# First feed-forward in plain float32: single products in place of high and low parts, and a fixed buffer for the routed up weights

## The chip, the cores and the metric

The kernel runs on one core of a Trainium2 chip. The metric is device time in microseconds (us); the time of a kernel is the median of its runs, and here there were three of the kernel before. The profile is one more execution, recorded by the hardware profiler.

## What is computed

Two transformer layers over 32 batches of 128 tokens with 128 features: cross-attention, then a feed-forward, twice. The change touches only the first feed-forward: a shared expert for every token, and eight routed experts of which each token uses the two with the highest scores.

```python
def _L0_ffn_ref(hidden_states, norm_weight, router_w, sw1, sb1, sw2, sb2, ew1, eb1, ew2, eb2):
    D, H, O, E, TOPK = (128, 512, 128, 8, 2)
    ...
    normed = hidden_states * jax.lax.rsqrt(var + 1e-08) * norm_weight
    shared = jnp.maximum(normed @ sw1 + sb1, 0.0) @ sw2 + sb2
    ...
    probs = jax.nn.sigmoid(flat @ router_w.T)
    scores, idx = jax.lax.top_k(probs, TOPK)
    w = scores / (jnp.sum(scores, axis=-1, keepdims=True) + 1e-06)
    ...
    h = jnp.maximum(jnp.einsum('td,edh->teh', flat, ew1) + eb1[None, :, :], 0.0)
    eo = jnp.einsum('teh,eho->teo', h, ew2) + eb2[None, :, :]
    routed = jnp.einsum('teo,te->to', eo, comb)
    return shared + routed.reshape(b, s, -1)
```

## The kernel before, in words

The program runs attention, the first feed-forward (`ffn0`, from L807), and then second attention and second feed-forward together. `P` is 128. The 32 batches form eight groups of four (512 tokens) and two halves of 16 batches. Each engine has its own block of code in `ffn0`, and semaphores order the engines; nothing reorders the instructions, so the order of an engine's work is the order of its code.

**Precision.** Each product of the feed-forward is three products of type float32r: `exact` (L1371) multiplies the high part of the weights by the high part of the data, low by high, and high by low. So each operand has to be split. ScalarE writes the high part (L1038 for weights, L1034 and L1096 for data, L1044 and L1111 for the hidden layer), and VectorE or GpSimd subtracts it from the whole for the low part (VectorE L1136 weights, L1259 and L1336 hidden layer, L1329 data of a block; GpSimd L967 data of a group). The weights come one expert after another through `w_in`, a buffer for two experts, so that SyncE's loads (L914) wait for VectorE's splits.

**Shared stage.** TensorE transposes a group (`transposes`, L1350), multiplies it by the shared up weights (`up`, L1381: a bias product and three of 512 columns for each of four slices of the hidden layer) and by the down weights (`down`, L1392: three of 512 columns each), then transposes the result back (`transpose_out`, L1404); VectorE adds it to `x` (`accumulate`, L1264). In the same stage the logits (L1367), the probabilities (ScalarE, L1060), the choice of two experts (VectorE `route`, L1159 to L1182), the place of each token in its expert's list (`prefix` on TensorE, `places` on VectorE, ending with the cast of `slots`, L1244) are made, once for each half. GpSimd makes the `scales` of a group (L959, L962) and scatters the normed rows into `xs` in DRAM, two indirect transfers a batch (L974); in its queue a group's scales stand behind three batches of scatters.

**Block stage.** 39 blocks of 128 rows for each half, 78 in all, each with one expert, whose number TensorE loads from `block_of` (L1478) to address the weights. SyncE loads blocks from `xs` in chunks of four. The loop of TensorE is four deep: transpose of block k (L1471), up of k-1 (bias L1481, three 512-column products L1483 to L1486), transposes of the hidden layer of k-2 (L1493), down of k-3 (four 256-column products L1504, a bias L1506, four 128-column products L1510). VectorE sums the two halves of the down product into `y_out` (L1343), and signals `by`. GpSimd scatters the second half while blocks of the first half run, each batch after a wait for `by` (L1011), and gathers the first half's results while blocks of the second half run, again each after a wait for `by` (L1018); VectorE adds them to `x` (L1311, L1316) at blocks that the list `ADD_AT` gives.

Of the kernel before, what the change touches and what calls it, by code (L numbers as in the profile page):

```python
# [89 lines left out]
class Kernel:  # L90
# [716 lines left out]
    def ffn0(self):  # L807
        nc, ps = self.nc, self.psum
        s = self.sems("f0", """small_in b2_rows sel tri iota b1_tr b2_tr b1_out b2_out b_hi b_rest b_mid b_low rows_zero
            rows_in w_hi w_lo stats mv veps scale xn xn_tr xT x_hi x_lo logit_mm prob  # L810
            top eq rank best m0 left m1 mask total rtot prefix scan small pos slot block_of
            s_rows up h_hi h_lo down out_copy out_tr acc
            bx_tr bx_hi bx_lo bup brelu bh_tr bh_hi bh_lo bdown by add0 add1""")
# [3 lines left out]
        experts_in = [self.sem(f"f0_experts_in{r}") for r in range(2)]  # L817
        UP_BANK, OUT_BANK, T_BANK, XT_BANK, PFX_BANK = 0, 4, 5, 6, 7
        U_BANKS, H_BANKS, X_BANKS, A_BANKS = (0, 1), (2, 3), (5, 6), (4, 7)
        XT_BANKS = (5, 4, 5, 4) + (XT_BANK,) * (G // 2)  # L820
        LOGIT_COL = 2 * E0 * HALF
        SH = E0
        W1_HI, W1_LO, W2 = 0, HID, 2 * HID
        xn = self.x_norm
        xT, outT = self.temp[:, 0:2], self.temp[:, 2]

        with ExitStack() as local:
# [4 lines left out]
            b2 = sb("b2", [NE, P])  # L832
            rw = sb("rw", [P, E0])
            nw = sb("nw", [P, 1])
            b2s = sb("b2s", [P, 1])
# [3 lines left out]
            b1_rows = sb("b1_rows", [P, E0, HID], BF16)  # L839
            b2_rows = sb("b2_rows", [P, E0, P], BF16)  # L840
            s_rows = sb("s_rows", [3, HID], BF16)
            sel3 = sb("sel3", [P, P], BF16)
            tri = sb("tri", [P, P], BF16)
# [28 lines left out]
            w_in = sb("w_in", [P, 2, 2, HID])  # L872
            ws_hi, ws_lo = (sb(f"ws_{n}", [P, 2, HID], F32R) for n in ("hi", "lo"))
            w = sb("w", [P, E0, 4 * HID], F32R)
            x_hi, x_lo = (sb(f"x_{n}", [P, G, GT], F32R) for n in ("hi", "lo"))
            h_hi, h_lo = (sb(f"h_{n}", [P, HB, GT], F32R) for n in ("hi", "lo"))
            hid = sb("hid", [P, HB, GT])
            chunks = xn[:, 0:CHUNKS_IN * CHUNK]
            y_out = hid[:, 2:4].rearrange("p r (c n) -> p (r c) n", n=P)
            xs_rows = self.xs[:].rearrange("(c p) d -> p c d", p=P)  # L880
            ys_rows = self.ys[:].rearrange("(c p) d -> p c d", p=P)

            def w_halves(e, k, lo):

                if e == SH:
                    return (ws_lo if lo else ws_hi)[:, k]
                if k == 0:
                    return w[:, e, lo * HID:(lo + 1) * HID]
                return w[:, e, W2:].rearrange("p (b h n) -> p h b n", b=HB, h=2)[:, lo]

            def w_raw(slot, e, k):
                if k == 1 and e != SH:
                    return w_in[:, slot, k].rearrange("p (b n) -> p b n", b=HB)
                return w_in[:, slot, k]

            order = (SH,) + tuple(range(E0))
            tiles = [slice(HALF * h, HALF * (h + 1)) for h in range(2)]
            yg = [t[:, 2:2 + G // 2].bitcast(F32).rearrange("p g (j n) -> p (g j) n", n=P) for t in (x_hi, x_lo)]

            with nc.Block() as block:  # L900
                @block.sync
                def _(sp):
                    for dst, name in ((b1[:], "f0_b1"), (b2[:], "f0_b2"), (rw[:], "f0_rw"), (nw[:], "f0_nw")):
                        sp.dma_start(dst, self.ins[name]).then_inc(s["small_in"], 16)
                    sp.dma_start(b_src[NE * HB:], self.ins["f0_b2"]).then_inc(s["b2_rows"], 16)
                    for n, e in enumerate(order):
                        if n == 2:
                            sp.wait_ge(s["b_low"], 1)
                            for part in range(3):
                                sp.dma_start(s_rows[part:part + 1], b_parts[E0 * HB:NE * HB, part]).then_inc(s["s_rows"], 16)  # L910
# [204 lines left out]
                def _(dve):  # L1115
# [162 lines left out]
                    for hb in range(HB):  # L1278
                        low(0, hb)
# [612 lines left out]
```

## Time and profile before

| | |
|---|---|
| median of 3 runs | 810.04 us (803.51 to 810.34) |
| span of the profiled execution | 837.9 us (its own time: the page gives the span alone) |
| TensorE busy | 740.8 us, 88% |
| VectorE busy | 537.9 us, 64% |
| ScalarE busy | 489.0 us, 58% |
| GpSimd busy | 311.8 us, 37% |
| first attention | 0 to 218.7 us |
| start of the feed-forward, to its first up product | 218.7 to 237.6 us |
| shared stage | 237.6 to 342.8 us |
| block stage | 342.8 to 553 us |
| second layer | 553 to 837.9 us |

The stage bounds were read from the timeline: an engine's busy time in a stage against the length of the stage tells whether it can be what bounds it. The granted clock of TensorE is told in shares of full speed. A plain float32 product shows up in the trace as two matmul records, a float32r or bfloat16 product as one. The length of a matmul record is modelled and overlaps the next; the price of a product is the step from its start to the next start.

### The profile page before, as it was taken

To read this page: it belongs to the slowest core of one execution; us is meant where nothing else is said; L and a number is where in the kernel's file an instruction comes from. 1 tells how busy PE (TensorE), PEld (TensorE's weight loads), DVE (VectorE), ACT (ScalarE), POOL (GpSimd) and SP (SyncE) were. 2 spreads that over 40 slices of the span, in tenths; PEclk is the share of its full clock that TensorE was granted. 3 is DMA by queue.
4 is the path that set the end of the run, shared out by engine and by line. 5 is a ranking of instruction groups with operands and counts; after the bars stand their busy time and mean duration, and the time that the engine had idled before them with its cause. 6 is when DMAs were issued, how large, how long until landed. Compare 5 with 4: busy or idle time off the path is not lost. (4 is left out here: it accounts for less than half of the span.)

```text
span 837.9 us, 19759 instructions
## 1 busy us (share of the span) xinstructions
PE 740.8 (88%) x6730; PEld 535.0 (64%) x6756; DVE 537.9 (64%) x1395; ACT 489.0 (58%) x792; POOL 311.8 (37%) x495
## 2 busy tenths in 40 slices
PE   6888999999787897899999999976688899997997
PEld 5555666666564564678788878865356566665553
DVE  6786887776546556545455456654678897766663
ACT  4466888888333353345555454653467788886442
POOL 5853554411253573145400545006655433122210
PEclk8998999999868799799999999999689999999899
DMA  7685765541101123022211333138645544510011
GB/s 213 93 157 106 122 120 106 107 87 33 53 25 47 47 89 111 20 83 83 80 52 48 83 83 82 31 94 139 126 83 103 95 90 78 93 23 2 14 39 50
DMA packets 72394, 66.78 MB, mean 80 GB/s; under 512 B 8138, under 2 KB 63340, under 8 KB 72044
## 3 DMA queue, kind: packets, MB, share of 16 engines
q1 hardware_dynamic: 57788, 51.88, 29.3%
q0 software_dynamic: 4096, 8.40, 3.7%
q10 hardware_dynamic: 10416, 5.25, 2.3%
q8 instruction: 59, 0.97, 0.5%
q14 instruction: 35, 0.29, 0.1%
HBM read 21.55 MB, written 16.65 MB: 46 GB/s over the span
## 5 line engine op out<-in xcount | busy, mean ns | idle before, releaser
L576 DVE TENSOR_REDUCE a_negmax<-psum 128x4 f32<-128x512 f32 x256 | 164.4, 685 | 7.9 <-PE psum L690 6.5
L443 ACT ACTIVATE temp<-psum 128x1024 f32<-128x1024 f32 x128 | 131.3, 1025 | 24.2 <-PE psum L708 18.8
L1336 DVE TENSOR_TENSOR f_h_lo<-psum,f_h_hi 128x512 fp32r<-128x512 f32 x78 | 53.9, 691 | 69.5 <-ACT f_h_hi L1111 53.7
L690 PE MATMUL psum<-a_k_stack,a_q_stack 96*128 96x256 bf16 x512 | 84.3, 282 | 8.1 <-DVE a_negmax L576 6.2
L974 POOL DMA_INDIRECT xs<-scratch,slots x64 | 63.0, 984 | 70.5 <-DVE f_hid L1343 54.5
L722 PE MATMUL psum<-temp,a_v_st 128*18 128x128 f32 x2048 | 82.4, 278 | 7.1 <-issue 3.1
L708 PE MATMUL psum<-a_q_stack,a_k_stack 128*128 128x128 bf16 x1024 | 80.7, 223 | 1.0 <-ACT temp L443 0.5
L377 POOL CAST a_nm_cols<-a_negmax 128x16 bf16<-128x16 f32 x64 | 13.6, 213 | 177.8 <-DVE a_negmax L576 177.2
L722 PEld LDWEIGHTS psum<-temp,a_v_st 128*18 128x18 f32 x2048 | 46.8, 98 | 49.8 <-issue 41.9
L708 PEld LDWEIGHTS psum<-a_q_stack,a_k_stack 128*128 128x128 bf16 x1024 | 66.2, 101 | 16.6 <-issue 15.7
L458 ACT ACTIVATE a_q_stack<-psum 32x1024 bf16<-32x1024 bf16 x64 | 65.1, 1017 | 11.6 <-PE psum L730 10.6
L1104 ACT ACTIVATE f_hid<-psum 128x512 f32<-128x512 f32 x78 | 46.7, 599 | 37.7 <-PE psum L1486 27.7
L668 PE MATMUL psum<-scratch,attn_w 128*128 128x512 f32 x96 | 55.2, 659 | 14.3 <-DVE a_rest_k L569 9.5
L1096 ACT ACTIVATE f_x_hi<-psum,f_nw 128x128 fp32r<-128x128 f32 x78 | 28.8, 370 | 62.7 <-PE psum L1471 54.0
L690 PEld LDWEIGHTS psum<-a_k_stack,a_q_stack 96*128 96x128 bf16 x512 | 44.8, 100 | 23.8 <-DVE a_negmax L576 14.1
L1504 PE MATMUL psum<-f_w,f_h_hi 128*128 x312 | 56.5, 303 | 0.0
L582 DVE TENSOR_TENSOR x<-psum,x 128x128 f32<-128x128 f32 x64 | 18.6, 290 | 58.9 <-PE psum L734 58.3
L1510 PE MATMUL psum<-f_w,f_h_lo 128*128 x312 | 50.3, 284 | 0.0
L1259 DVE SCALAR_TENSOR_TENSOR f_h_lo<-psum,f_h_hi 128x512 fp32r<-128x512 f32 x32 | 22.1, 696 | 42.3 <-ACT f_h_hi L1044 26.7
L1493 PE MATMUL psum<-ident,f_hid 128*128 128x128 f32 x312 | 47.7, 276 | 1.4 <-ACT f_hid L1104 1.2
L1044 ACT ACTIVATE f_h_hi<-psum 128x512 fp32r<-128x512 f32 x32 | 19.1, 596 | 50.4 <-PE psum L1375 43.4
L1483 PE MATMUL psum<-f_w,f_x_hi 128*128 x78 | 43.9, 562 | 5.0 <-ACT f_x_hi L1096 4.2
(234 smaller groups left out, 1699.3 us busy)
## 6 DMA issues: line engine op xcount, KB each, us to landing
a_k_stack<-a_k_parts SPq DMA_DIRECT2D x192, 64.0 KB
a_q_stack<-a_q_parts SPq DMA_DIRECT2D x96, 128.0 KB
xs<-zeros ACTq DMA_DIRECT2D x8, 640.0 KB, 5.1
f_w_in<-in_f_w SPq DMA_DIRECT2D x18, 256.0 KB
scratch<-xs SPq DMA_DIRECT2D x18, 256.0 KB
ys<-f_hid SPq DMA_DIRECT2D x18, 256.0 KB
scratch<-in_ctx SPq DMA_DIRECT2D x16, 256.0 KB
x<-in_x SPq DMA_DIRECT2D x8, 256.0 KB, 6.0
```

The lines of the kernel that those rows point to most:

```text
L443: nc.scalar.activation(pt[:, unit].rearrange("p a b t -> p (a b t)"), ps[:, bank:bank + 2].rearrange("p a n -> p (a n)"), ACT.Exp, scale=S ...
L458: nc.scalar.activation(rows, nm_psum[STACK_ROWS:P].unsqueeze(1).to_broadcast([MAX_ROWS, BLK, P]), ACT.Copy).then_inc(s["nm_out"], 1)
L576: nc.vector.tensor_reduce(negmax[:, b % 2, :, 2 * unit:2 * unit + 2].rearrange("p n b -> p b n"), ps[:, P1_BANK + unit % 2].rearrange("p ( ...
L668: nc.tensor.matmul(ps[:, A_BANK], weights[w][swapped], (self.xT, self.cT)[w][:, g % 2], start=True, stop=True).then_inc(s["mm_" + qk[w]], 1)
L690: last = nc.tensor.matmul(ps[:, P1_BANK + unit % 2, 2 * j * P:2 * (j + 1) * P], q_cols(b, blk, STACK_ROWS), k_cols(b, blk, STACK_ROWS, sli ...
L708: last = nc.tensor.matmul(ps[:, p2_bank(b, half) + par, bass.ts(j, P)], k_cols(b, blk, P, par), q_cols(b, blk, P), start=True, stop=True)
L722: last = nc.tensor.matmul(ps[32 * j:32 * j + V_COLS, PV_BANK, bass.ts(half, P)], v_st[:, b % 2, c0:c0 + V_COLS], pt[:, half, par, j], star ...
L974: pool.indirect_dma_start(self.xs[:], bass.IndirectOffsetOnAxis(self.slots[:, b, n:n + 1], 0), xn[:, b], None,).then_inc(self.scattered[h] ...
L1336: nc.vector.tensor_tensor(h_lo[:, n % 2], ps[:, H_BANKS[n % 2]], h_hi[:, n % 2], ALU.subtract,).then_inc(s["bh_lo"], 1)
L1493: last = nc.tensor.transpose(ps[:, H_BANKS[k % 2], bass.ts(hb, P)], hid[:, k % 2, bass.ts(hb, P)], self.ident[:])
L1504: nc.tensor.matmul(bank[:, 0:2 * P], h_hi[:, k % 2, bass.ts(hb, P)], w[:, e, c:c + 2 * P], start=hb == 0, stop=False)
L1510: last = nc.tensor.matmul(bank[:, 0:P], h_lo[:, k % 2, bass.ts(hb, P)], w[:, e, c:c + P], start=False, stop=hb == HB - 1)
```

## The change

All operands of the first feed-forward stay whole, and each product is one plain float32 product. With the splits go the buffers for parts, the two-expert buffer `w_in`, ScalarE's and VectorE's and GpSimd's splitting, the transposes of the hidden layer and those of the shared result. In the shared stage the up product keeps its form (the weights stationary, 512 tokens moving), the bias moves into ScalarE's pass, and the down product takes a slice of the hidden layer as stationary and 128 columns of the weights as moving, which leaves the result untransposed. In the block stage both products have stationary operands of 128x128 and 128 moving columns: in the up product the expert's weights are stationary, and as they are chosen by number, VectorE first copies them into a fixed buffer `bw` (two deep); in the down product the hidden layer is stationary and the weights, addressed by number, are moving. The biases of the block's hidden layer come by a product of `b1_cols` and `sel12`. The loop is three deep, not four. The waits for `by` ahead of each scatter and gather are gone, `ADD_AT` is set later, and SyncE loads all weights without a wait, behind 27 small loads of biases.

```diff
                     def up(g, hb):
...
-                        nc.tensor.matmul(bank, s_rows[:, bass.ts(hb, P)], ones, start=True, stop=False)
-                        exact(bank, ws_hi[:, 0, bass.ts(hb, P)], ws_lo[:, 0, bass.ts(hb, P)],
-                              x_hi[:, g], x_lo[:, g], False, True).then_inc(s["up"], 1)
+                        nc.tensor.matmul(ps[:, UP_BANK + hb], w1[:, SH, bass.ts(hb, P)], xT[:, g], start=True, stop=True,
+                                         ).then_inc(s["up"], 1)
                     def down(g, hb):
...
                         for j in range(GB):
-                            last = nc.tensor.transpose(ps[:, T_BANK, bass.ts(j, P)], outT[:, bass.ts(j, P)], self.ident[:])
-                        last.then_inc(s["out_tr"], 1)
+                            last = nc.tensor.matmul(ps[:, bank, bass.ts(j, P)], h[:, g % 2, hb, bass.ts(j, P)],
+                                                    w2[:, SH, bass.ts(hb, P)], start=False,
+                                                    stop=hb == HB - 1 and j == GB - 1)
+                        last.then_inc(s["down"], 1)
...
                     def block_up(k):
...
-                        nc.tensor.matmul(bank, sel3[:], b1_rows[:, e], start=True, stop=False)
-                        pe.wait_ge(s["bx_hi"], k + 1)
-                        nc.tensor.matmul(bank, x_hi[:, k % 2, 0:P], w[:, e, W1_HI:W1_HI + HID], start=False, stop=False)
-                        nc.tensor.matmul(bank, x_hi[:, k % 2, 0:P], w[:, e, W1_LO:W1_LO + HID], start=False, stop=False)
-                        pe.wait_ge(s["bx_lo"], k + 1)
-                        nc.tensor.matmul(bank, x_lo[:, k % 2, 0:P], w[:, e, W1_HI:W1_HI + HID], start=False, stop=True,
-                                         ).then_inc(s["bup"], 1)
+                        wait(pe, s["bh"], k - 1)
+                        nc.tensor.matmul(bank, b1_cols[:, e], sel12[:].rearrange("p a n -> p (a n)"), start=True, stop=False)
+                        pe.wait_ge(s["bxT"], k + 1)
+                        pe.wait_ge(s["bw"], k + 1)
                         for hb in range(HB):
+                            last = nc.tensor.matmul(bank[:, bass.ts(hb, P)], bw[:, k % 2, bass.ts(hb, P)], bxT[:, k % 2],
+                                                    start=False, stop=hb == HB - 1)
+                        last.then_inc(s["bup"], 1)
                     def block_down(k):
...
                         for hb in range(HB):
-                            c = W2 + 2 * P * hb
-                            last = nc.tensor.matmul(bank[:, 0:P], h_lo[:, k % 2, bass.ts(hb, P)], w[:, e, c:c + P],
+                            last = nc.tensor.matmul(bank, h[:, k % 2, 0, bass.ts(hb, P)], w2[:, e, bass.ts(hb, P)],
                                                     start=False, stop=hb == HB - 1)
                         last.then_inc(s["bdown"], 1)
...
+                    def block_weights(k):
...
+                        e = dve.value_load(block_of[0:1, slot:slot + 1], min_val=0, max_val=E0 - 1)
+                        wait(dve, s["bup"], k - 1)
+                        nc.vector.tensor_copy(bw[:, k % 2], w1[:, e]).then_inc(s["bw"], 1)
...
+                    for k in range(NBLK + 4):
+                        if 0 < k + 1 < NBLK:
+                            block_weights(k + 1)
...
-                            nc.vector.tensor_reduce(y_out[:, slot_of(n) % (CHUNK * CHUNKS_OUT)],
-                                                    ps[:, A_BANKS[n % 2], 0:2 * P].rearrange("p (h n) -> p n h", h=2),
-                                                    AX, ALU.add).then_inc(s["by"], 1)
+                            nc.vector.tensor_copy(y_out[:, slot_of(n) % (CHUNK * CHUNKS_OUT)],
+                                                  ps[:, Y_BANKS[n % 2], 0:P]).then_inc(s["by"], 1)
...
                     for b in range(HALF, B):
-                        pool.wait_ge(s["by"], 1 + 3 * (b - HALF) // 2)
                         scatter(b)
...
                     for b in range(HALF):
-                        pool.wait_ge(s["by"], HBLK + 3 + 3 * b // 2)
                         for n in range(2):
```

TensorE's queue in the steady part of the block stage holds for one block, before:

```order
L1471 MATMUL psum<-ident,scratch 128x128
L1478 TENSOR_LOAD f_block_of
L1478 ISA x2
L1481 ISA
L1481 MATMUL psum<-f_b_rows,f_sel 128x512
L1483 ISA
L1483 MATMUL psum<-f_w,f_x_hi 128x512
L1484 ISA
L1484 MATMUL psum<-f_w,f_x_hi 128x512
L1486 MATMUL psum<-f_w,f_x_lo 128x512
L1493 MATMUL psum<-ident,f_hid 128x128 x4
L1504 ISA
```

Behind these stand the 256-column down products with an address step each, the bias and four 128-column products. After, the same place of the same queue reads:

```order
L1366 MATMUL psum<-ident,scratch 128x128
L1373 TENSOR_LOAD f_block_of
L1373 ISA x2
L1376 ISA
L1376 MATMUL psum<-f_sel,f_b_cols 128x512
L1380 MATMUL psum<-f_bxT,f_bw 128x128 x4
L1390 REGISTER_ALU
L1390 MATMUL psum<-f_b_rows,f_sel 128x128
L1393 ISA
L1393 MATMUL psum<-f_w,f_h 128x128
```

The pair of the last two rows comes four times. Gone are the 512-column products of the data and the transposes of the hidden layer between up and down.

VectorE's queue around the first half's routing in the shared stage (the split of the shared weights, four norms, the split of a group's hidden layer, the choice of the first expert), before:

```order
L1136 TENSOR_TENSOR f_ws_lo<-f_w_in,f_ws_hi 128x512 x2
L1130 TENSOR_SCALAR scratch<-x,f_mv,f_scale 128x128 x8
L1259 SCALAR_TENSOR_TENSOR f_h_lo<-psum,f_h_hi 128x512 x4
L1159 TENSOR_REDUCE f_top<-f_prob 128x16
L1161 TENSOR_TENSOR attn_w<-f_prob,f_top 128x128
```

And after:

```order
L1059 BN_STATS f_bn<-x 128x6 x4
L1063 BN_AGGR f_mv<-f_bn 128x2 x4
L1071 TENSOR_SCALAR scratch<-x,f_mv,f_scale 128x128 x8
L1095 TENSOR_REDUCE f_top<-f_prob 128x16
L1097 TENSOR_TENSOR attn_w<-f_prob,f_top 128x128
```

The routing follows the norms at once; the split of the hidden layer that stood ahead of it is no longer there.

In the block stage VectorE has, for one block, after:

```order
L1243 TENSOR_LOAD f_block_of
L1243 ISA x2
L1245 ISA
L1245 COPY f_bw<-f_w 128x512
L1261 COPY f_y_out<-psum 128x128
```

The copy of the weights for block k+1 stands ahead of the copy of the result of block k-2.

## Rows read from the trace of the kernel before

**Rows 1.** The page, its first line.

```profile
span 837.9 us, 19759 instructions
```

**Rows 2.** Busy times by stretch: start:end, length, PE, PEld, DVE, ACT, POOL (instructions), PEclk, DMA share, GB/s.

```profile
237.60:342.80 105.20, 86.88 (x326) 54.71 (x325) 62.10 (x174) 40.38 (x69) 48.08 (x47) 0.84 0.19 58
342.80:553.00 210.20, 203.34 (x1378) 174.72 (x1404) 110.46 (x266) 109.25 (x234) 61.39 (x64) 0.99 0.23 65
```

**Rows 3.** Timeline of PE, one undisturbed block: start us, length us, engine, line, operation.

```profile
441.69 0.30 PE L1471 MATMUL psum<-ident,scratch 128*128 128x128 f32 x1
441.85 0.58 PE L1483 MATMUL psum<-f_w,f_x_hi 128*128 x1
442.27 0.39 PE L1484 MATMUL psum<-f_w,f_x_hi 128*128 x1
442.50 0.39 PE L1486 MATMUL psum<-f_w,f_x_lo 128*128 x1
...
443.69 0.64 PE L1510 MATMUL psum<-f_w,f_h_lo 128*128 x4
444.17 0.30 PE L1471 MATMUL psum<-ident,scratch 128*128 128x128 f32 x1
```

**Rows 4.** Timeline of PE: plain float32 products elsewhere in the kernel.

```profile
104.75 0.44 PE L734 MATMUL psum<-attn_w,a_yT 128*128 128x128 f32 x2
105.02 0.49 PE L690 MATMUL psum<-a_k_stack,a_q_stack 96*128 96x256 bf16 x3
...
105.52 1.11 PE L674 MATMUL psum<-attn_w,scratch 128*128 128x128 f32 x8
106.46 0.38 PE L743 MATMUL psum<-ident,a_u 128*128 128x128 f32 x2
...
800.62 1.98 PE L1771 MATMUL psum<-a_f_xT,a_f_w1s 128*128 128x512 f32 x4
802.44 0.38 PE L183 MATMUL psum<-ident,a_f_outT 128*128 128x128 f32 x2
```

**Rows 5.** Busy times by stretch, line L1483 alone: PE, PEld (x blocks).

```profile
350.45:415.59 65.14, 12.94 (x24) 4.52 (x24) 1.00 0.26 75
423.85:466.01 42.16, 9.81 (x17) 3.23 (x17) 1.00 0.23 63
```

**Rows 6.** Groups by line and form: busy us, mean ns, idle before.

```profile
L1104 ACT ACTIVATE f_hid<-psum 128x512 f32<-128x512 f32 x78 | 46.7, 599 | 37.7 <-PE psum L1486 27.7 <-remote 8.9 <-issue 1.1
L1343 DVE TENSOR_REDUCE f_hid<-psum 128x128 f32<-128x256 f32 x78 | 32.6, 417 | 19.3 <-remote 11.9 <-PE psum L1510 5.5 <-issue 1.9
L674 PEld LDWEIGHTS psum<-attn_w,scratch 128*128 128x128 f32 x128 | 16.6, 200 | 2.9 <-ACT scratch L418 1.6 <-issue 1.0
```

**Rows 7.** Line L1478: duration ns min/median/max, first and last start.

```profile
L1478 PEldq TENSOR_LOAD <-f_block_of x78: 295/302/493, 342.8 to 545.6; - x78
L1478 PEldq FUSED_REGOPS  x78: 151/151/165, 343.4 to 546.0; - x78
```

**Rows 8.** Timeline of DVE, first half's routing and places, their first and last operations.

```profile
247.86 0.28 DVE L1159 TENSOR_REDUCE f_top<-f_prob 128x16 f32<-128x128 f32 x1
...
251.41 0.71 DVE L1182 TENSOR_TENSOR f_mask<-f_m 128x128 bf16<-128x128 f32 x1
...
256.90 0.41 DVE L1203 TENSOR_TENSOR_SCAN attn_w<-psum,zero 128x128 f32<-128x128 f32 x1
...
260.74 0.18 DVE L1244 CAST slots<-f_slotf 128x32 uint32<-128x32 f32 x1
```

**Rows 9.** Timeline of DVE and POOL: scatters beside a split.

```profile
311.16 0.68 DVE L1136 TENSOR_TENSOR f_w<-f_w_in,f_w 128x512 fp32r<-128x512 f32 x1
311.41 1.27 POOL L974 DMA_INDIRECT xs<-scratch,slots  x1 [0.31 <-issue]
312.99 0.96 POOL L974 DMA_INDIRECT xs<-scratch,slots  x1 [0.30 <-issue]
314.25 0.96 POOL L974 DMA_INDIRECT xs<-scratch,slots  x1 [0.30 <-issue]
```

**Rows 10.** Timeline of ACT in the block stage, behind a burst of scatters.

```profile
358.42 0.37 ACT L1096 ACTIVATE f_x_hi<-psum,f_nw 128x128 fp32r<-128x128 f32 x1 [2.39 <-remote]
```

More of the change, by code:

```diff
@@ new lines, in _ @@
+                    sp.dma_start(w1[:, SH], self.ins["f0_w1"][:, SH]).then_inc(s["sw_in"], 16)
+                    sp.dma_start(w2[:, SH], self.ins["f0_w2"][:, SH]).then_inc(s["sw_in"], 16)
+                    sp.wait_ge(s["b_low"], 1)
+                    sp.wait_ge(s["rows_zero"], 2)
+                    for part in range(3):
+                        sp.dma_start(b2_rows[part:part + 1].rearrange("o e n -> o (e n)"), b_parts[NE * HB:, part]
+                                     ).then_inc(s["b2_in"], 16)
@@ new lines, in _ @@
+                    for part in range(3):
+                        for e in range(E0):
+                            sp.dma_start(b1_cols[HB * part:HB * (part + 1), e], b_parts[HB * e:HB * (e + 1), part]
+                                         ).then_inc(s["b1_in"], 16)
+                    for e in range(E0):
+                        sp.dma_start(w1[:, e], self.ins["f0_w1"][:, e]).then_inc(s["w_in"], 16)
+                        sp.dma_start(w2[:, e], self.ins["f0_w2"][:, e]).then_inc(s["w_in"], 16)
@@ new lines, in _ @@
+                    scales(2)
+                    pool.wait_ge(s["tri"], 2)
+                    nc.gpsimd.affine_select(out=tri[:], in_=tri[:], compare_op=ALU.is_ge, fill=0.0, base=-1,
+                                            pattern=[[1, P]], channel_multiplier=-1).then_inc(s["tri"], 1)
+                    pool.wait_ge(s["iota"], 2)
+                    nc.gpsimd.tensor_scalar(rev[:], iota_i[:], -1.0, float(E0), ALU.mult, ALU.add,
+                                            ).then_inc(s["iota"], 1)
@@ new lines, in _ @@
+                    nc.gpsimd.tensor_copy(starts[:], starts_i[:]).then_inc(s["iota"], 1)
+                    scales(3)
+                    for part in range(3):
+                        pool.wait_ge(s["sel"], 3 + part)
+                        nc.gpsimd.affine_select(out=sel12[:], in_=sel12[:], compare_op=ALU.not_equal, fill=1.0,
+                                                base=-HB * part, pattern=[[-1, HB], [0, P]], channel_multiplier=1,
+                                                ).then_inc(s["sel"], 1)
@@ L1046, in copy_out, with hidden @@
[L1046 to L1052 removed]
+                    def hidden(g, hb):
+                        act.wait_ge(s["up"], HB * g + hb + 1)
+                        wait(act, s["down"], HB * (g - 2) + hb + 1)
+                        nc.scalar.activation(h[:, g % 2, hb], ps[:, UP_BANK + hb], ACT.Relu,
+                                             bias=b1[:, SH * HB + hb:SH * HB + hb + 1]).then_inc(s["h"], 1)
@@ L1087, in _ @@
-                        if g == G // 2 + 1:
-                            probabilities(1)
-                    for k in range(NBLK + 2):
+                            hidden(g + 1, 0)
+                            hidden(g + 1, 1)
+                        if 0 < g <= G // 2 - 1:
+                            copy_xT(G // 2 + g - 1)
+                        if g == 5:
+                            probabilities(1)
+                        if g + 1 < G:
+                            hidden(g + 1, 2)
+                            hidden(g + 1, 3)
@@ L1400, in transpose_out @@
[L1400 to L1408 removed]
+                            pe.wait_ge(s["b2_in"], 16 * 3)
```

423 lines of the change are left out of this document (138 added, 285 removed).

## The prediction

> **What bounds the kernel now.** I read the busy times by stretch first. The span is 837.9 us [rows 1], and the change touches two stretches of it: the stage with the shared expert, 105.20 us, in which TensorE is busy for 86.88 us at a mean granted clock of 0.84, and the stage with the 78 routed blocks, 210.20 us, with TensorE busy for 203.34 us at 0.99 [rows 2]. So the block stage is bound by TensorE: what a block costs there is what its products cost. In the shared stage some 18 us of TensorE's time are waits, and part of the rest runs at the lower level of the clock, so there the waits count, not the products.
>
> Next comes TensorE's timeline over one undisturbed block [rows 3]. A start-to-start step is the price: 0.16 us for the transpose, 0.42 for the bias together with the first 512-column product, 0.23 for each further one (so 0.19 to 0.21 for the bias), and 2.48 us from one block's transpose to the next. 17 blocks at this pace take 42.16 us; while GpSimd issues its indirect transfers, 24 blocks take 65.14 us, or 2.71 each [rows 5]. 78 x 2.48 is 193.4 us, which leaves 16.8 us of the stage for these disturbances and for filling and draining.
>
> **Blocks: the products.** Away go three 512-column products, four transposes of the hidden layer and the two-part down products. New are four up and four down products in plain float32, each of 128 columns with weights of its own. A plain product stands in the trace as two records. Four of the same shape step from 105.52 to 106.46 (L674): 0.94 us, 0.1175 a record. One alone (L734) takes 0.27 us, 0.135 to 0.14 a record [rows 4]. I take L674, whose four follow each other as here. A block then costs 0.16 + 0.20 (bias, 512 columns) + 0.94 + 0.05 (second bias, a quarter of the columns of the first) + 0.94 = 2.28 us with rounding, 0.20 less than now: 78 x 0.20 = 15.6 us less. Bounds: 0.11 a record (2.16 us a block, 25 us less) to 0.14 (2.70, 17 us more).
>
> The risk is the weight load. The loads of L674 take 200 ns each by their records [rows 6], yet eight of them and their products fit in 0.94 us, so they lie largely beside products. The Trainium skill, "TensorE: Matmul & The Clock Gate", section The mechanism, states that weight loads overlap products in flight only when the row group differs; all products here use the whole array, so by that rule each load would stand in the open. The eight records of L674 speak against it. What it would cost is the second rival.
>
> **Blocks: the other engines.** VectorE loses both splits and gains, per block, a load of the expert's number and the copy of 128x512 weights. A load of the same number on TensorE's queue takes 302 ns, an address step 151 [rows 7]; with gaps 0.65 us. The copy is bounded by 0.28 us (an operation on 128 columns, L1159 [rows 8]) and 0.68 (the split of as many elements, L1136 [rows 9]); I take 0.68. The result's copy replaces a reduction of 0.42 us [rows 6] and is counted as that. With 0.2 us for handing over that is 1.95 us, under 2.28, so TensorE covers it; the copy for block k+1 is asked for as soon as the up products of block k-1 end, about 3.6 us ahead of its use. Only where the first half's sums are added (some 26 blocks with one more operation on 128 columns each, 0.29 to 0.42 us) do the two come level: 0.1 us over, 3 us in all. ScalarE keeps one of two passes of 0.60 us [rows 6] and a short copy: covered. The 16.8 us of filling and disturbance I keep as they are; bounds 6 us (no disturbance) and 30.
>
> **Shared stage.** Products: 32 plain 512-column ups at 0.91 (L1771: four records, two products, step 1.82 us [rows 4]), 29 us, and 128 short downs at 0.235, 30 us, with 13 for transposes, logits and biases: about 72 us, not much less than the products of now. That gives nothing. The gain lies in what no longer waits. Queued on VectorE behind splits are now the routing, the norms and the results. Step by step:
> - Routing of the first half begins at 247.86 now, and the mask is done 4.3 us later [rows 8]. Without splits ahead of it, by a count of the four norms, transposes and logits from the stage's start at 218.7, I put its start at 239 (bounds 233, and 247.9 for no gain): mask 243.3; the prefix product stands behind the first group's downs (245.8), and the places take 4.0 us [rows 8]: slots at 250.1 instead of 260.9.
> - From there GpSimd paces: three blocks of scatters are six transfers 1.26 us apart [rows 9], 7.6 us, and the next group's scales about 1.5 behind them: 9.1 us a group, three times: the last scales at 277.8, the transpose of the last group at 279.5.
> - Behind it, TensorE has 4.6 us left of group 4's turn, 8.6 us for the next (four ups 3.64, four downs of four products 3.76, bias 0.2, logits 0.96) and 7.6 for the one behind it: 300.3. The second half's prefix 0.3, its places 4.0, block numbers and gates 1, two accumulations 1.4 and the first weights' copy with its number 1.3 make 308.3: first up product of a block.
> Now the stage begins at 342.8 [rows 2], and its first up product comes a microsecond later: 35.5 us less. Bounds: only the slots' 10.8 us remain (the clock at its lower level, other waits), or TensorE alone sets the stage (first up product at 230, 72 us, the last step of 3: 305, 39 us less). The scatters of the second half, 32 x 1.26 = 40 us, end near 345, before block 31 (about 379) needs them. The routed weights, 16 transfers of 256 KB, wait for nobody any more, where a buffer two experts deep holds them up now; no stall is counted for them.
>
> **Sum.** 15.6 + 35.5 - 3 = 48 us off the profiled execution, to 790. The profiled 837.9 us are 27.9 above the runs' median of 810.04; scaled by 810.04/837.9 = 0.967 it is 46 us: **764 us**. With 25 + 39 and 10 of disturbance gone, 74 x 0.967 = 72: 738 us.
>
> **Rivals.**
> 1. *Signals come late while GpSimd issues without a pause.* Now its transfers are paced, four at a time, and in a burst ScalarE starts 2.39 us late with a releaser that the trace doesn't know [rows 10]; a burst costs 0.23 x 3 = 0.7 us on TensorE [rows 5]. After, both waits on finished blocks are gone and 64 transfers come in two stretches of 40 us. If every block in them then takes 3.4 us (2.28 and half of such a wait), 24 blocks lose 27 us, and the 11 us of present bursts go (24 x 0.23 for the scatters, as much for the gathers): 48 + 11 - 27 = 32, 31 scaled: 779. For it: the wait rows. Against: the shared stage has such bursts too, and in the list of waits between 262 and 324 us none has an unknown releaser.
> 2. *Slower: float32 weight loads stand in the open.* 78 x 16 block records and 256 in the shared downs are 1504. The gain of 48 us is used up at 48/1504 = 0.032 above 0.1175, that is 0.149 us a record: from there on the change loses. At 0.14 (L734) it gains 14, 796. If a load of 0.19 to 0.20 had to end before its product starts, 0.19: 109 us more, 869 us. For it: L734, one product alone, is dearer than four, and in the new down products each weight comes from an address in a register. Against: the eight records of L674, and the register steps are hidden now.
> 3. *VectorE paces the blocks.* If the load of the expert's number drains VectorE, its 1.95 us grow. At 2.75 a block 37 us of the 48 are gone: 799; at 2.90 there is no change. For it: no number is loaded on VectorE in the trace. Against: 0.8 us have to be found.
> 4. *Scatters slowed by VectorE's copies.* One transfer beside a split (L1136) took 1.27 instead of 0.96 us [rows 9]: 32 x 0.3 = 10 us, the second half is in place at 355 instead of 345, still in time. The Trainium skill, "SBUF — State Buffer", section SBUF: two separate sides, holds that a float32 copy within SBUF locks GpSimd out of a shared port, so that such a transfer takes 3100 instead of 620 ns. The row shows a tenth of that. As a mechanism of this kernel: at 3.1 us or more from one transfer to the next, 32 take 99 us, the second half stands at 403, 24 us after block 31 wants it: 48 - 24 = 24, 787. It decides from 2.3 us a transfer.
>
> **Chances.** Forecast 0.53; rival 1 0.15; rival 2 0.18 (0.15 of it slower than before); rival 3 0.08 (half of it no change); rival 4 0.06. A measurement of this kernel tells about 1%, 8 us, from no change. Faster by more: 0.53 + 0.15 + 0.02 + 0.02 + 0.05 = 0.77, taken as 0.76; within: 0.07; slower: 0.17. The likeliest case alone runs from 742 to 785 us. To hold the time 8 times in 10 the range takes in rivals 1, 3 and 4 and the near part of rival 2: 738 to 818 us; left out are the costly half of rival 2 and little below.
>
> **What would show it.** Right: a block's transpose-to-transpose step of 2.2 to 2.35 us outside the bursts; four ups in 0.94 us; the slots' cast near 250; the first block's up products near 308; VectorE idle in each block. Wrong: steps of a plain product's record at 0.15 us and more (rival 2); TensorE waiting for the weights' copy in the steady part (rival 3); waits with an unknown releaser over both 40 us stretches (rival 1); a wait of the transpose at the second half's first block (rival 4); the slots' cast still behind 258 us, which takes the shared stage's term away.

## The result, and the profile after

The median of the kernel after is 761.31 us (757.6 to 765.32, 4 runs) against 810.19 for the kernel before (4 runs): a ratio of 0.940, 95% interval 0.934 to 0.946, 49 us less. The forecast was 764.

The profiled execution of the kernel after lasts 763.6 us; that run, at 765.32 us, is the slowest of the four, 0.5% above the median. TensorE's share of the span rises from 88% to 90%. The lines of the page that answer to the one of [rows 1], and the first engine row:

```profile
span 763.6 us, 19550 instructions
PE 687.0 (90%) x6885; PEld 522.2 (68%) x6885; DVE 458.2 (60%) x1267; ACT 437.5 (57%) x679; POOL 299.6 (39%) x491
```

Busy times by stretch of the kernel after, same columns as [rows 2]: the shared stage from the first up product to the last down product, the block stage, the second layer.

```profile
228.70:309.40 80.70, 71.32 (x414) 52.87 (x414) 30.45 (x123) 27.62 (x42) 39.24 (x45) 0.94 0.27 89
309.40:488.30 178.90, 175.16 (x1485) 170.84 (x1483) 67.78 (x200) 75.04 (x156) 61.71 (x64) 0.99 0.26 77
488.30:763.60 275.30, 238.15 (x2578) 157.22 (x2578) 195.18 (x546) 178.32 (x260) 95.03 (x184) 0.94 0.35 77
```

In the shared stage TensorE now idles 9 us, where it idled 18 (a wait of 3.35 us, shown below, lies just behind this stretch), and its mean granted clock is 0.94, not 0.84. The first up product begins at 228.7 us, where it began at 237.6 [rows 2]: about 9 of the 30 us by which the block stage starts earlier lie ahead of the shared stage's products. The block stage is still TensorE's, 175 of 179 us. Its timeline over one block, which answers to [rows 3]:

```profile
420.30 0.27 PE L1366 MATMUL psum<-ident,scratch 128*128 128x128 f32 x1
420.41 0.38 PE L1376 MATMUL psum<-f_sel,f_b_cols 128*128 128x512 bf16 x1
420.63 1.05 PE L1380 MATMUL psum<-f_bxT,f_bw 128*128 128x128 f32 x8
421.52 0.22 PE L1390 MATMUL psum<-f_b_rows,f_sel 128*128 x1
421.58 1.11 PE L1393 MATMUL psum<-f_w,f_h 128*128 x8
422.52 0.27 PE L1366 MATMUL psum<-ident,scratch 128*128 128x128 f32 x1
```

A block costs 2.22 us: transpose 0.11, bias 0.22, four up products 0.89, second bias 0.06, four down products 0.94. The eight records of the up products step 0.111 us each, a little under L674's 0.1175 [rows 4].

The path to the block stage in the shared stage: the timelines of DVE and PE at the places where something waits. The number in brackets is the idle time ahead of the row, with what ended it.

```profile
249.06 0.18 DVE L1180 CAST slots<-f_slotf 128x32 uint32<-128x32 f32 x1
...
259.18 1.18 DVE L1071 TENSOR_SCALAR scratch<-x,f_mv,f_scale 128x128 f32<-128x128 f32 x4 [6.70 <-POOL f_scale L932]
...
261.41 0.66 DVE L1194 TENSOR_TENSOR x<-psum,x 128x512 f32<-128x512 f32 x1
...
277.10 1.18 DVE L1071 TENSOR_SCALAR scratch<-x,f_mv,f_scale 128x128 f32<-128x128 f32 x4 [6.07 <-POOL f_scale L932]
```

```profile
224.21 0.66 PE L1271 MATMUL psum<-ident,scratch 128*128 128x128 f32 x4 [0.82 <-DVE scratch L1071]
...
235.70 2.14 PE L1284 MATMUL psum<-f_rw,f_xT 128*128 128x8 f32 x16
...
262.32 0.59 PE L1302 MATMUL psum<-f_b_rows,f_sel 128*128 128x512 bf16 x1 [6.71 <-DVE x L1194]
262.70 1.92 PE L1306 MATMUL psum<-f_w,f_h 128*128 128x128 f32 x8
264.41 1.91 PE L1292 MATMUL psum<-f_xT,f_w 128*128 128x512 f32 x2
...
285.43 0.60 PE L1271 MATMUL psum<-ident,scratch 128*128 128x128 f32 x4
...
313.45 1.13 PE L1380 MATMUL psum<-f_bxT,f_bw 128*128 128x128 f32 x8 [3.35 <-DVE f_bw L1245]
```

The slots are cast at 249.06, where the forecast had 250.1. Then comes a wait that it hadn't: the third group's down product needs the memory bank that holds the first group's result, VectorE empties it (L1194) at 261.41, and ahead of that in VectorE's queue stands a norm that waits 6.70 us for GpSimd's scales. Behind this wait four products step 1.71 us (262.70 to 264.41) instead of 0.89; the granted clock from 262.70 to 266.12 us is 0.50, the lower of its two levels. A second wait, 3.35 us for the copy of the first block's weights, stands just ahead of the block stage.

### The profile page after: what moved, and what is told of

The parts are those of the page before. It is cut to its first block and busy times, and to the rows that moved or that the text cites. A ratio compares the mean times of both kernels' runs of the same rounds, so it can differ in the third digit from the quotient of the medians.

```text
span 763.6 us, 19550 instructions
## 1 busy us (share of the span) xinstructions
PE 687.0 (90%) x6885; PEld 522.2 (68%) x6885; DVE 458.2 (60%) x1267; ACT 437.5 (57%) x679; POOL 299.6 (39%) x491
## 5 line engine op out<-in xcount | busy, mean ns | idle before, releaser
L443 ACT ACTIVATE temp<-psum 128x1024 f32<-128x1024 f32 x128 | 131.0, 1024 | 19.4 <-PE psum L708 13.2
L1393 PE MATMUL psum<-f_w,f_h 128*128 x624 | 87.4, 284 | 0.0
L1380 PEld LDWEIGHTS psum<-f_bxT,f_bw 128*128 128x128 f32 x624 | 82.6, 193 | 6.5 <-issue 3.7
L1380 PE MATMUL psum<-f_bxT,f_bw 128*128 128x128 f32 x624 | 83.1, 277 | 3.3 <-DVE f_bw L1245 3.3
L1051 ACT ACTIVATE f_h<-psum 128x512 f32<-128x512 f32 x78 | 46.6, 597 | 62.2 <-PE psum L1380 62.2
L1245 DVE COPY f_bw<-f_w 128x512 f32 x78 | 34.1, 437 | 79.2 <-PE psum L1380 79.2
L377 POOL CAST a_nm_cols<-a_negmax 128x16 bf16<-128x16 f32 x64 | 13.6, 212 | 170.9 <-DVE a_negmax L576 170.7
L939 POOL DMA_INDIRECT xs<-scratch,slots x64 | 62.2, 972 | 39.9 <-DVE slots L1180 21.3
L1393 PEld LDWEIGHTS psum<-f_w,f_h 128*128 128x128 f32 x624 | 76.7, 194 | 0.9
L989 POOL DMA_INDIRECT f_xT<-ys,slots x32 | 30.7, 960 | 64.2 <-DVE f_y_out L1261 54.8
L1043 ACT ACTIVATE f_bxT<-psum,f_nw 128x128 f32<-128x128 f32 x78 | 28.6, 367 | 42.8 <-PE psum L1366 42.8
L1004 ACT ACTIVATE f_h<-psum,f_b 128x512 f32<-128x512 f32 x32 | 22.0, 687 | 47.4 <-PE psum L1292 47.4
```

The costliest lines, as they stand in the source:

```text
L443: nc.scalar.activation(pt[:, unit].rearrange("p a b t -> p (a b t)"), ps[:, bank:bank + 2].rearrange("p a n -> p (a n)"), ACT.Exp, scale=S ...
L939: pool.indirect_dma_start(self.xs[:], bass.IndirectOffsetOnAxis(self.slots[:, b, n:n + 1], 0), xn[:, b], None,).then_inc(self.scattered[p] ...
L1051: nc.scalar.activation(h[:, n % 2, 0], ps[:, U_BANKS[n % 2]], ACT.Relu).then_inc(s["bh"], 1)
L1245: nc.vector.tensor_copy(bw[:, k % 2], w1[:, e]).then_inc(s["bw"], 1)
L1380: last = nc.tensor.matmul(bank[:, bass.ts(hb, P)], bw[:, k % 2, bass.ts(hb, P)], bxT[:, k % 2], start=False, stop=hb == HB - 1)
L1393: last = nc.tensor.matmul(bank, h[:, k % 2, 0, bass.ts(hb, P)], w2[:, e, bass.ts(hb, P)], start=False, stop=hb == HB - 1)
```

## The experiments

All edits are to the kernel before or to the kernel after, as said. Their times are given as ratios to the kernel before on the same chip.

**The kernel before, once more.** No edit.

> The kernel before, once more with a profile. Its first profiled execution took 837.9 us, 27.9 over the median of its runs, and lost time in the block stage (16.8 us beside 78 x 2.48) and in the unchanged second layer (284.9 us against 275.3 after the change). Theory A, that execution was a slow one and not typical: span 803 to 816 us, block stage 195 to 202 us with hardly any wait of unknown releaser, second layer 274 to 278 us. Theory B, the waits belong to the kernel whenever it is profiled: span 830 to 840 us, again one long block in three during the transfers, second layer near 285.

Measured: span 818.5 us. Three rows of its busy times by stretch, the last for line L1471 alone, PE and PEld (x blocks):

```profile
237.60:342.50 104.90, 85.98 (x330) 54.31 (x329) 62.21 (x174) 40.47 (x69) 48.22 (x48) 0.84 0.19 59
546.00:818.50 272.50, 238.32 (x2557) 156.68 (x2555) 193.49 (x544) 176.32 (x260) 94.06 (x180) 0.94 0.37 76
...
350.00:415.00 65.00, 7.72 (x26) 3.64 (x26) 1.00 0.28 81
```

Theory A holds in kind. 26 blocks start in the 65 us in which 24 took 65.14 [rows 5]: the long blocks are gone though GpSimd issues as before, and its list of waits has none of unknown releaser. The shared stage is the same, so that part of the first profile stands. The span and the second layer are 1 to 3 us above what theory A gave. This execution is the better one to set beside the kernel after. First and last rows of its block stage:

```profile
343.47 0.91 PE L1483 MATMUL psum<-f_w,f_x_hi 128*128 x1 [0.44 <-ACT f_x_hi L1096]
...
539.12 0.42 DVE L1343 TENSOR_REDUCE f_hid<-psum 128x128 f32<-128x256 f32 x1 [0.42 <-PE psum L1510]
```

From it the 54.9 us between the two spans divide so: first up product of a block at 313.45 instead of 343.47, 30.0 us; from there to the end of the last block's result 174.8 us (to 488.24) instead of 196.1 (to 539.54), 21.3 us; the rest, whose code is the same, 275.4 instead of 279.0, 3.6 us.

**Before, unpaced.** The two waits ahead of GpSimd's transfers taken out:

```diff
-                        pool.wait_ge(s["by"], 1 + 3 * (b - HALF) // 2)
...
-                        pool.wait_ge(s["by"], HBLK + 3 + 3 * b // 2)
```

> The kernel before without GpSimd's waits for finished blocks ahead of each batch of scatters and of gathers; nothing else changed. Theory A, the paced bursts make the long blocks: blocks at 2.48 us throughout, 8 to 11 us less than the kernel before, ratio 0.986 to 0.990. Theory B, the transfers disturb the split scheme whether paced or not: the same number of long blocks, packed into two stretches, ratio 0.997 to 1.003. Theory C, transfers without a pause hold ScalarE and VectorE up more: 10 to 20 us more, ratio 1.012 to 1.025.

Measured: ratio 0.996 (0.993 to 1.000). Blocks at 2.48 us throughout, among GpSimd's transfers too (PE's timeline, two starts of L1469):

```profile
372.41 0.30 PE L1469 MATMUL psum<-ident,scratch 128*128 128x128 f32 x1
374.89 0.30 PE L1469 MATMUL psum<-ident,scratch 128*128 128x128 f32 x1
```

The time is that of theory B, the blocks are those of theory A: in the kernel as it runs there was next to nothing to win, since with the pace there are no long blocks either. Theory C, the first rival of the prediction, falls.

**After, paced.** The same two waits put back into the kernel after.

> The kernel after, with the two waits for finished blocks put back. Theory A, the paced bursts make the long blocks: with them some 16 blocks of the 78 grow from 2.22 to about 3 us, 8 to 11 us more than after, 770 to 772 us. Theory B, a block of the new form has enough slack on ScalarE and VectorE: blocks stay at 2.22 us, 759 to 764 us.

Measured: 765.4 us, where the kernel before takes 813.7 on this chip: ratio 0.937 (0.931 to 0.942), within the interval of the kernel after; blocks still at 2.22 us (332.81 to 335.02 in PE's timeline, and so throughout). Theory B.

```profile
332.81 0.27 PE L1368 MATMUL psum<-ident,scratch 128*128 128x128 f32 x1
...
335.02 0.27 PE L1368 MATMUL psum<-ident,scratch 128*128 128x128 f32 x1
```

So taking the waits out gave the change nothing that these intervals show, and cost nothing.

**After, accumulations first.**

```diff
                     for g in range(G):
+                        if g == 1:
+                            accumulate(0)
+                        if g == 2:
+                            accumulate(1)
                         if g < 3:
                             norm(4 + g)
...
-                        if g > 0:
+                        if g > 2:
                             accumulate(g - 1)
```

> The kernel after, with VectorE's accumulation of groups 0 and 1 ahead of the norms of groups 5 and 6 that wait for GpSimd. Theory A, that order made TensorE wait 6.71 us for the accumulation and explains the 5 us by which the block stage begins later than forecast: first up product of a block at 307 to 310 instead of 313.45, 755 to 757 us. Theory B, the next transpose then waits for the same norm: at most 2 us less, 759 to 761 us.

Measured: ratio 0.934 (0.930 to 0.939), not told apart from the kernel after. The executions begin the feed-forward at different times, so I count from the first group's transpose: first up product of a block 91.0 us later (220.17 to 311.12), in the kernel after 89.2 (224.21 to 313.45). Of the 91.0, 2.0 are lost before any of the waits in question: from that transpose up to the logits of the third and fourth group this execution takes 13.46 us at a granted clock of 0.73, the kernel after 11.49 us at 0.85.

```profile
220.17 0.79 PE L1275 MATMUL psum<-ident,scratch 128*128 128x128 f32 x4 [0.28 <-DVE scratch L1071]
...
277.01 0.59 PE L1306 MATMUL psum<-f_b_rows,f_sel 128*128 128x512 bf16 x1 [4.63 <-DVE x L1194]
```

The wait has moved by two groups, from the third group's down product to the fifth's: the third accumulation stands behind the last norm, and the last norm behind GpSimd. Theory A fails as it was put: the order of two instructions doesn't explain the wait, since another order only moves it. Theory B is right on the total alone, which gains nothing: the transposes wait 1.09 and 0.18 us for their norms, and the long wait is again that for an accumulation. What is left to explain the wait is GpSimd's pace (three batches of scatters ahead of each group's scales); the run with the scales first tests that.

**After, unchanged**, beside the next three.

> The kernel after, unchanged, on the same chip as the three that follow. Expected again 757 to 768 us, shared stage and blocks as in its first profile (first up product of a block at 311 to 315 us, blocks at 2.22 us).

Measured: 762.11 us, ratio 0.942 (0.936 to 0.947). First transpose to first up product of a block 89.0 us (218.53 to 307.51): the span differs by 3.8 us from the first profile, this distance by 0.2. The feed-forward begins 5.7 us earlier in this execution, so the block is below the 311 to 315 us expected. The wait for the accumulation is 5.05 us here in place of 6.71, since products ahead of it step slower (an up product 1.71 us, 247.25 to 248.96); it ends 38.15 us behind the first transpose (256.68), in the first profile 38.11 (262.32).

**After, scales first.** The point that the accumulations left open. GpSimd:

```diff
-                    scales(G // 2)
+                    for g in range(G // 2, G):
+                        scales(g)
                     pool.wait_ge(self.cleared_rows, 16 * G)
...
                         scatter(b)
-                        g = G // 2 + 1 + (b - 2) // 3
-                        if (b - 2) % 3 == 0 and b >= 2 and g < G:
-                            scales(g)
```

VectorE, the order of its calls: statistics of groups 4 to 7, `route(0)`, `norm(4)`, `places(0)`, `block_experts(0)`, `norm(5)` to `norm(7)`, then the accumulations; `block_weights(0)` and `block_weights(1)` behind `route(1)`, and `gates()` at the end.

> The kernel after in another order: GpSimd makes the scales of groups 4 to 7 ahead of the first half's scatters (VectorE their statistics ahead of the routing), the norms follow without a wait, and VectorE copies the weights of the first two blocks ahead of the second half's places. Theory A, GpSimd's pace is what the shared stage waits for: TensorE's wait of 6.7 us goes, the wait of 3.35 us for the first weights too, first up product of a block at 302 to 305 instead of 313.45, 8 to 10 us less than after, 751 to 754 us. Theory B, TensorE's own products and the clock set the stage by now: at most 3 us less.

Measured: 746.95 us, ratio 0.921 (0.917 to 0.926), 15 us under the kernel after on the same chip. PE's timeline, and the busy times of its shared stage:

```profile
231.38 2.14 PE L1283 MATMUL psum<-f_rw,f_xT 128*128 128x8 f32 x16
...
249.88 0.38 PE L1301 MATMUL psum<-f_b_rows,f_sel 128*128 128x512 bf16 x1 [1.35 <-DVE x L1192]
...
295.50 1.16 PE L1379 MATMUL psum<-f_bxT,f_bw 128*128 128x128 f32 x8 [0.35 <-ACT f_bxT L1041]
```

```profile
227.80:294.80 67.00, 65.53 (x407) 49.77 (x406) 26.80 (x106) 26.28 (x40) 35.34 (x39) 0.99 0.32 107
```

TensorE idles 1.5 us in the stage and runs at 0.99. From the logits of the third and fourth group to the first up product of a block it is 64.1 us (231.38 to 295.50), in the kernel after 77.8 (235.70 to 313.45): 13.6 less. The waits that went make up 10.9 us of it (2.54 ahead of the fifth group's transpose, 6.71 less 1.35, 3.35 less 0.35), and the products behind the 6.71 us, which stepped at the lower clock there, some 2. Theory A names the cause; the gain is larger than its 8 to 10 us. What is left of the 15 us lies within the interval. This version beats both kernels.

**After, without the copy of the up weights.** The up product takes expert 0's weights in every block, so the choice of the expert is left out there:

```diff
-                        e = dve.value_load(block_of[0:1, slot:slot + 1], min_val=0, max_val=E0 - 1)
-                        wait(dve, s["bup"], k - 1)
-                        nc.vector.tensor_copy(bw[:, k % 2], w1[:, e]).then_inc(s["bw"], 1)
...
-                            last = nc.tensor.matmul(bank[:, bass.ts(hb, P)], bw[:, k % 2, bass.ts(hb, P)], bxT[:, k % 2],
+                            last = nc.tensor.matmul(bank[:, bass.ts(hb, P)], w1[:, 0, bass.ts(hb, P)], bxT[:, k % 2],
```

> The kernel after without the copy of the expert's up weights: each block's up product uses the weights of expert 0, so the choice of the expert is left out there. Theory A (forecast), TensorE hides VectorE's load and copy: blocks stay at 2.22 us, only the wait of 3.35 us ahead of the first block goes: 2 to 4 us less than after. Theory B (VectorE paces): blocks at 2.1 us or less, over 9 us less.

Measured: ratio 0.939 (0.933 to 0.945), so nothing that could be told from the kernel after. Blocks at 2.22 us as in theory A; the wait of 3.35 us is gone.

```profile
421.38 0.27 PE L1363 MATMUL psum<-ident,scratch 128*128 128x128 f32 x1
...
423.60 0.27 PE L1363 MATMUL psum<-ident,scratch 128*128 128x128 f32 x1
```

**After, three more copies in each block.** They go to a buffer that nothing reads:

```diff
                         nc.vector.tensor_copy(bw[:, k % 2], w1[:, e]).then_inc(s["bw"], 1)
+                        for n in range(3):
+                            wait(dve, s["spare"], n + 3 * k - 2)
+                            nc.vector.tensor_copy(spare[:, n], w1[:, n]).then_inc(s["spare"], 1)
```

> The kernel after with three further copies of 128x512 on VectorE behind each block's copy of the weights, into a buffer that nothing reads: 3 x 0.43 = 1.3 us more in a block, where VectorE idled 1.5 of 2.22 us. Theory A, all of that idle time is usable: blocks stay at 2.22 us, total within 3 us of after. Theory B, loading the expert's number keeps VectorE from copying (0.5 us by the queue's rows) and counts too: blocks at 2.4 to 2.6 us, 12 to 28 us more than after.

Measured: ratio 0.936 (0.930 to 0.943), blocks at 2.22 us (422.07 to 424.29). VectorE still waits for TensorE ahead of each copy of weights:

```profile
423.60 0.43 DVE L1246 COPY f_bw<-f_w 128x512 f32 x1 [0.49 <-PE psum L1384]
423.94 1.29 DVE L1249 COPY f_spare<-f_w 128x512 f32<-128x512 f32 x3
...
425.81 0.43 DVE L1246 COPY f_bw<-f_w 128x512 f32 x1 [0.39 <-PE psum L1384]
```

```profile
422.07 0.27 PE L1370 MATMUL psum<-ident,scratch 128*128 128x128 f32 x1
...
424.29 0.27 PE L1370 MATMUL psum<-ident,scratch 128*128 128x128 f32 x1
```

Theory A: the third rival had over 1.3 us of VectorE's time a block to go. The same run weighs the fourth: with four copies in a block, half of GpSimd's 32 scatters of the block stage take 1.05 to 1.08 us, the others about 0.96; of its gathers, three take 1.74 to 1.76 us, where none of the kernel after takes more than 1.07.

```profile
331.08 1.08 POOL L940 DMA_INDIRECT xs<-scratch,slots  x1 [0.30 <-issue]
...
434.71 1.76 POOL L990 DMA_INDIRECT f_xT<-ys,slots  x1 [0.30 <-issue]
```

**After, down weights at a fixed address.** The down product takes expert 0's weights in every block, so the choice of the expert is left out there.

```diff
-                            last = nc.tensor.matmul(bank, h[:, k % 2, 0, bass.ts(hb, P)], w2[:, e, bass.ts(hb, P)],
+                            last = nc.tensor.matmul(bank, h[:, k % 2, 0, bass.ts(hb, P)], w2[:, 0, bass.ts(hb, P)],
```

> The kernel after with the down product of each block taken with the weights of expert 0 at a fixed address, so that the choice of the expert is left out there. The four down products step 0.95 us, the four up products, whose addresses are fixed, 0.89. Theory A, the address from a register costs that difference: four downs in 0.89, blocks at 2.16 us, about 4.5 us less than after. Theory B, it comes from the change to the next accumulation or operand, not from the address: blocks unchanged at 2.22 us.

Measured: ratio 0.940 (0.934 to 0.945), four downs in 0.94 us as before. Theory B; addresses from a register cost nothing that these steps show. What makes four downs 0.05 us longer than four ups wasn't tried.

```profile
422.33 0.27 PE L1366 MATMUL psum<-ident,scratch 128*128 128x128 f32 x1
...
424.55 0.27 PE L1366 MATMUL psum<-ident,scratch 128*128 128x128 f32 x1
```

**Before, routing first.**

```diff
+                    route(0)
                     for hb in range(HB):
                         low(0, hb)
-                    route(0)
```

> The kernel before with one part of the change alone: VectorE routes the first half ahead of the split of group 0's hidden layer instead of behind it. Theory A, the place of the routing in VectorE's queue is worth by itself what its earlier end is: slots 4 to 5 us earlier, 3 to 5 us less than before. Theory B, TensorE's downs want that split and wait instead, and the prefix stands behind them: slots at most 2 us earlier, total within 2 us of before or slower.

Measured: ratio 1.005 (1.001 to 1.010). From the first transpose the slots' cast begins 37.1 us later (218.59 to 255.67); in the first profile it was 34.5 (226.25 to 260.74). TensorE's first down product now waits for the split:

```profile
218.59 1.11 PE L1354 MATMUL psum<-ident,scratch 128*128 128x128 f32 x4 [1.95 <-DVE scratch L1130]
...
240.47 0.77 PE L1375 MATMUL psum<-f_h_hi,f_ws_hi 128*128 128x512 f32 x1 [1.55 <-DVE f_h_lo L1259]
```

```profile
255.67 0.18 DVE L1244 CAST slots<-f_slotf 128x32 uint32<-128x32 f32 x1
```

Theory B. With the splits in place, moving the routing gives nothing: the prefix stands behind the downs, and these behind the splits.

## Why the prediction was right, point by point

**The sum** was right: 46 us forecast, 49 measured (ratio 0.940, where 764/810 is 0.943). That it came so close is in part luck. Set beside the repetition of the kernel before, the blocks gave 21.3 us where 15.6 less 3 stood in the sum, and the shared stage 30.0 where 35.5 stood: two errors of 9 and 5.5 us in opposite directions, 51.3 us in place of 48. Another 3.6 us of the two spans' difference lie in the second layer, whose code is the same.

**Blocks: 15.6 us forecast, 21.3 measured.** The step named was right: plain products of 128 columns with weights of their own follow each other as L674's do. The size was 0.1175 us a record, measured 0.111 (up) and 0.118 (down), and 0.11 for the transpose instead of 0.16: 2.22 us a block instead of 2.28. (The upper bound was added up wrongly: with 0.14 a record the terms give 2.65 us a block, 13 us more, not 2.70 and 17. The forecast doesn't rest on it.) The 3 us that I set aside for VectorE where it adds the first half's sums weren't needed: its copy of the weights takes 0.43 us, where I took 0.68, and the result's copy 0.29, where I took 0.42 (groups by line and form, block stage):

```profile
L1245 DVE COPY f_bw<-f_w 128x512 f32 x78 | 34.1, 437 | 79.2 <-PE psum L1380 79.2
L1261 DVE COPY f_y_out<-psum 128x128 f32<-128x128 f32 x78 | 22.7, 291 | 31.7 <-PE psum L1393 31.7
```

**The 16.8 us of filling and disturbance, "I keep as they are".** This step failed. The profiled execution of the kernel before had long blocks among the transfers that its repetition doesn't have. Of the 19.4 us between the two executions, 13 lie in the block stage: L1343's last row ended at 552.96 in the first and at 539.54 in the second, and the stage began 0.4 us apart. The kernel after has none: 174.8 us for 78 blocks of 2.22, or 173.2. What those waits of unknown releaser were stays open. In that one execution the long blocks stand only where GpSimd issues transfers [rows 5]; that its pace is enough to make them is refuted, since the repetition with the pace and the run without it show none. On the forecast the step cost little: the 16.8 us stood in the time before and in the time after alike, and only the scaling by 0.967 took 2 us off the difference.

```profile
552.53 0.43 DVE L1343 TENSOR_REDUCE f_hid<-psum 128x128 f32<-128x256 f32 x1 [0.42 <-PE psum L1510]
```

**Shared stage: 35.5 us forecast, 30.0 measured.** The count from the stage's start to the slots (250.1, measured 249.06) and GpSimd's 9.1 us a group were right: its scales follow each other by 8.96 us in the trace. The failing step is "Behind it, TensorE has 4.6 us left of group 4's turn": TensorE wasn't there yet. It had waited 6.71 us in the third group's turn for an accumulation that stands in VectorE's queue behind a norm, had lost some 2 us more to the lower clock behind that wait, and so reached the last group's transpose at 285.4, not 279.5, though VectorE was done with that group's norm at 278.3. I had followed the transposes' waits and not the accumulations', though both are in the same queue. The remaining steps (8.6, 7.6, the places, the copy) hold to within a microsecond. That it was GpSimd's pace behind the wait is shown by the run with the scales first, and not by the one with the accumulations first, where it only moved.

"That gives nothing. The gain lies in what no longer waits" holds in part. The stage between its first up product and its last down product shrank by 24.5 us, and TensorE's idle time in it by 9. The unit of two products in slices (up and down of one slice) costs 1.75 us after (L1292 from 238.80 to 240.55, shown at the end) and cost 1.90 before (L1388 from 252.45 to 254.35), 5 us over 32 units: the products did give something. The other ten go with a granted clock of 0.94 in place of 0.84 and with the transposes of the result that are gone; they weren't measured apart. The routing's place alone isn't worth the 10.8 us of earlier slots, by the run that moved it alone. That the splits had to go for them is read from the queues; no run takes the splits out by themselves.

**Rivals.** 1 (late signals): refuted by the kernel before without its pace, and by the trace of the kernel after, whose list of waits has none of unknown releaser in the feed-forward. 2 (weight loads in the open): the profile refutes it; 0.111 us a record, with a load of 0.19 us for each, leaves no room for loads in the open, and the run with fixed addresses takes its second argument away. The Trainium skill's sentence that weight loads overlap products in flight only when the row group differs ("TensorE: Matmul & The Clock Gate", The mechanism) doesn't hold as it stands for these rows, nor did it for L674's; the same section lets a load for the background weight buffer go ahead too, and with that these rows agree. 3 (VectorE paces): refuted, with over 1.3 us a block to spare. 4 (locked scatters): one copy a block leaves the scatters at a median of 0.96 us; with four, half of them take up to 1.08 and three gathers up to 1.76, none 3.1. The second half's blocks start without a wait. What the Trainium skill says of such a transfer ("SBUF — State Buffer", SBUF: two separate sides) isn't seen at that size here.

```profile
L1380 PEld LDWEIGHTS psum<-f_bxT,f_bw 128*128 128x128 f32 x624 | 82.6, 193 | 6.5 <-issue 3.7
```

```profile
L939 POOL DMA_INDIRECT xs<-scratch,slots x64: 954/958/1217, 250.2 to 350.2; - x64
```

## What to carry to other kernels

A plain float32 product is worth trying against three products of parts: its two records of 0.11 us for 128 columns cost TensorE a tenth less a block here, and it takes the splits off the engines whose queues hold the rest up. A count of one chain is only as good as the list of what the same queue must do in between: follow each engine's queue, and ask of every instruction behind a waiting one who needs it. Profile the kernel before twice before its waits are put into a sum: the second profile here had none of the long blocks of the first.

## What was not expected of the hardware

Four products of 128 columns, eight records with eight loads of weights, cost 0.89 us; one of 512 columns, two records with two loads, 0.86 (L1292, 238.80 to 239.66): six more loads, 0.19 us each by their records, cost 0.03. A wait of 6.71 us at TensorE cost more than itself: the four products behind it stepped 1.71 us instead of 0.89, the next product of 512 columns 1.71 instead of 0.86, at a granted clock of 0.50, the lower of its two levels, and the stage lost about 2 us to that. Three further copies on VectorE in each block, 1.3 us of work, changed nothing that the blocks' steps show.

```profile
238.80 1.02 PE L1292 MATMUL psum<-f_xT,f_w 128*128 128x512 f32 x2
239.66 1.05 PE L1306 MATMUL psum<-f_w,f_h 128*128 128x128 f32 x8
240.55 1.02 PE L1292 MATMUL psum<-f_xT,f_w 128*128 128x512 f32 x2
```
